# Four attention layers over one adjacency: packing two chunks of signs in one run of TensorE

## What is computed

```python
def _L0_gnn_ref(h, adj, W, a):
    Wh = h @ W
    e = (Wh @ a1)[:, None] + (Wh @ a2)[None, :]
    e = jnp.where(e >= 0, e, ALPHA * e)
    scores = jnp.where(adj > 0, e, NEG_BIG)
    attention = jax.nn.softmax(scores, axis=1)
    return attention @ Wh
...
h = jnp.maximum(_layernorm(x, axis=-1), 0.0)
x = x + _L0_gnn_ref(h, adj, L0_gnn_W, L0_gnn_a)
```

## Time and profile before

| | us |
|---|---|
| median of 3 runs (lowest, highest) | 3853.71 (3852.88, 3855.01) |
| span of the profiled execution | 3851.4 |
| a group of layer 0, pack to pack | 61.05 |
| a group of layer 1, projection to projection | 58.08 |

### The profile page before, as it was taken

One profiled execution on the slowest core, in us unless ns is written; L12 is line 12 of the kernel. 1 busy time (PEld: TensorE's weight loads), 2 busy tenths in 40 slices (PEclk: granted clock), 3 DMA queues, 4 the chain that ended last, 5 costly groups with the idle time before them and its releaser, 6 DMA issues.

```text
span 3851.4 us, 82260 instructions
## 1 busy us (share of the span) xinstructions
PE 3814.9 (99%) x34730; PEld 3789.4 (98%) x34730; DVE 3583.9 (93%) x7818; ACT 1234.0 (32%) x2601; POOL 56.0 (1%) x155
## 2 busy tenths in 40 slices
PE   7999999999999999999999999999999999999999
PEld 7999999999999999999999999999999999999999
DVE  7998999999999999999999999999997999999998
ACT  6777777777631111111133221121123000000000
POOL 4100000000000000000000000000000000000000
PEclk9999999999999999999999999999999999999999
DMA  7988888898300100010002000000000000000000
GB/s 245 303 290 296 295 293 291 289 301 293 127 17 19 18 23 18 18 22 19 15 15 67 18 20 21 18 20 20 18 18 16 15 15 15 15 18 12 15 18 9
DMA packets 223265, 344.00 MB, mean 89 GB/s; under 512 B 72496, under 2 KB 147632, under 8 KB 222896
## 3 DMA queue, kind: packets, MB, share of 16 engines
q1 hardware_dynamic: 221168, 338.48, 28.0%
q10 hardware_dynamic: 1728, 0.27, 0.0%
HBM read 305.70 MB, written 21.20 MB: 85 GB/s over the span
## 4 chain that ended last, share of the span: by engine, by line
PE 96%; DVE 2%; ACT 1%; DMA 1%; issue 1%; DVEq 0%; POOL 0%; ACTq 0%; SPq 0%
PE acc L1360 93%; PE ps_wh L1378 1%; DVE q L855 1%; PE ps_pack L1258 1%; DMA adj_int<-in_adj_dram 0%; ACT adj_pairs L1475 0%; PE ps_pack L1360 0%; DVE mask L799 0%; DMA vals<-in_x_dram 0%; PE acc L1342 0%; PE ps_pack L1244 0%; DVE q L663 0%; PE acc L1288 0%; ACT xnew L1597 0%; PE ps_pack L1265 0%
## 5 line engine op out<-in xcount | busy, mean ns | idle before, releaser
L1360 PE MATMUL acc<-vals,q 128*128 128x129 f32 (+1 forms) x32576 | 3665.7, 275 | 2.4 <-DVE q L855 2.3
L1360 PEld LDWEIGHTS acc<-vals,q 128*128 128x128 f32 x32576 | 3648.5, 192 | 15.3 <-issue 7.5
L855 DVE SCALAR_TENSOR_TENSOR q<-rrow,R,mask 128x512 f32<-128x512 f32 x3968 | 2890.6, 747 | 146.3 <-PE acc L1360 39.5
L1475 ACT ACTIVATE adj_pairs<-adj_int,threshold 128x1024 uint8<-128x1024 int32 x512 | 585.0, 1145 | 214.5 <-PE ps_pack L1258 133.8
L799 DVE TENSOR_SCALAR mask<-bits 128x512 uint16<-128x512 uint16 x2048 | 546.0, 285 | 2.9 <-ACT bits L1485 2.9
L1597 ACT ACTIVATE xnew<-acc,rec 128x128 f32<-128x128 f32 x244 | 69.3, 366 | 862.6 <-DVE rec L893 767.7
L1622 ACT ACTIVATE e<-xnew,nm,rs 128x128 f32<-128x128 f32 x193 | 79.6, 482 | 230.3 <-DVE nm L655 229.5
L1604 ACT ACTIVATE e<-xnew 128x512 f32<-128x512 f32 x47 | 29.6, 631 | 367.7 <-DVE xnew L924 279.7
L1675 ACT ACTIVATE wh<-ps_wh 128x512 f32<-128x512 f32 x48 | 28.7, 598 | 355.0 <-PE ps_wh L1378 354.1
L1617 ACT ACTIVATE sd<-ve 128x4 f32<-128x4 f32 x47 | 9.5, 201 | 353.3 <-DVE ve L635 353.3
L924 DVE SCALAR_TENSOR_TENSOR xnew<-mean,none,xnew 128x128 f32<-128x128 f32 x188 | 64.9, 345 | 47.4 <-ACT xnew L1597 47.4
(11 more groups left out here) (257 smaller groups left out, 829.6 us busy)
## 6 DMA issues: line engine op xcount, KB each, us to landing
adj_int<-in_adj_dram SPq DMA_DIRECT2D x512, 512.0 KB, 4.8
rrow<-rows SPq DMA_DIRECT2D x60, 256.0 KB, 3.3
x_between_layers<-xnew SPq DMA_DIRECT2D x32, 256.0 KB, 2.6
xin<-x_between_layers SPq DMA_DIRECT2D x32, 256.0 KB, 2.8
xin<-in_x_dram SPq DMA_DIRECT2D x16, 256.0 KB, 5.3
wh_of_layer<-wh SPq DMA_DIRECT2D x1, 4096.0 KB, 16.7
x_of_layer<-xnew SPq DMA_DIRECT2D x16, 256.0 KB, 2.3
xin<-x_of_layer SPq DMA_DIRECT2D x16, 256.0 KB, 3.2
```

What stands on the lines that cost most here:

```text
L855: nc.vector.scalar_tensor_tensor(q[:, j % RING, :], row, column(R_, t), mask[:, c % 2, j, :], ALU.max, ALU.mult).then_inc(q_ready, 1)
L1360: last = nc.tensor.matmul(to, q[:, j % RING, b * P:(b + 1) * P], vals[:, t, 0:width(g.layer)], start=first, stop=(t == KT - 1 or g.two and ...
L1475: nc.scalar.activation(adj_bytes[:, n % BIN_RING // 2, :, n % 2], adj_int[:, n % ADJ_RING, :], ACT.Sign, bias=threshold[:, 0:1], accum_out ...
```

## The change

- The ring of signs holds 16 pieces (`BIN_RING`). Odd chunks put theirs into the second half of `mask`, even ones into `adj_pairs` (`pairs_of`). Layer 0's mask has only buffer 0 (`plane_buffer`), so `unpack` also waits until VectorE's own last q is done.
- In groups 1 to 14 of layer 0 TensorE packs two chunks in one run: behind t = 19 chunks 2 and 3 of the group, behind t = 51 chunks 0 and 1 of the next (`RUNS_AT`). Even ones write the bank `ps_pack`, odd ones `ps_bc` (`words_bank`). Group 0 and group 15 pack singly.
- ScalarE copies both chunks' words one behind the other, at i = 0 and i = 16. VectorE turns even chunks at t % 16 == 15, right ahead of their planes, and odd ones at 12 as before.
- In layer 0, but for its last group, `normalised` moves from i = 21 to 23, `copy_hT` from 27 to 28, `copy_wh` from 30 to 31, and TensorE's projection from t = 57 to 50. On SyncE the transposing transfer moves from 25 to 27 and the next rows from 27 to 29.

```diff
-BIN_RING = 8
+BIN_RING = 16
+WORDS_AT = {0: (1, 12, 20, 28), 1: (4, None, None, None), LAST: (None, 12, 20, None)}
+FIRST_SINGLE = GROUPS * CHUNKS - 2
+RUNS_AT = {19: 2, 51: 4}
+RUN_TURN_AT = JC - 1
...
+        def words_bank(C):
+            return ps_bc if C % 2 and FIRST_TURNED <= C < FIRST_SINGLE else ps_pack
...
+        pairs_of = [flat(adj_pairs), flat(mask).bitcast(F16)[:, JC * W // 2:JC * W]]
...
-                    if before and i == 25:
+                    if before and i == 27:
                         turn_halves(before)
-                    if before and i == 27:
+                    if before and i == 29:
                         load_next_rows(before)
...
+                need(dve, q_ready, (g.swept * CHUNKS + c) * JC)
+                planes(bits[:, g.value, c * JC:(c + 1) * JC, :], plane_buffer(g, c)).then_inc(mask_ready, 1)
...
+                        at = RUN_TURN_AT if C % 2 == 0 and C < FIRST_SINGLE else TURN_AT
+                        if FIRST_TURNED <= C < CHUNKS * GROUPS and t % JC == at:
                             turn_words(C)
...
-                need(pe, words_copied, C - FIRST_TURNED)
+                need(pe, words_copied, C - FIRST_TURNED - (C <= FIRST_SINGLE))
...
+                    if g.layer == 0 and 0 < g.value < LAST and t in RUNS_AT:
+                        C = g.value * CHUNKS + RUNS_AT[t]
+                        pack(C // CHUNKS, C % CHUNKS)
+                        pack((C + 1) // CHUNKS, (C + 1) % CHUNKS)
...
-                        if t == (39 if g.two else 57):
+                        if t == (39 if g.two else 50 if g.layer == 0 and not g.last else 57):
                             project(before)
...
+                C = v * CHUNKS + n // QP
+                if n % QP == QP - 2:
+                    need(act, words_turned, C - 1 - FIRST_TURNED)
...
+                    later = g.layer == 0 and not into_last
-                    due.append((2 * QP + 5, lambda: normalised(g)))
-                    due.append((3 * QP + 3, lambda: copy_hT(g)))
-                    due.append((3 * QP + 6, lambda: copy_wh(g)))
+                    due.append((2 * QP + (7 if later else 5), lambda: normalised(g)))
+                    due.append((3 * QP + (4 if later else 3), lambda: copy_hT(g)))
+                    due.append((3 * QP + (7 if later else 6), lambda: copy_wh(g)))
...
+                        if i == 0 and g.value > 1 or i == 2 * QP and 0 < g.value < LAST:
+                            for c in range(2):
+                                words(g.value, i // QP + c)
```

More of the change, by code:

```diff
@@ L804, in planes, with plane_buffer @@
                 return last
+            def plane_buffer(g, c):
+                return 0 if g.layer == 0 else c % 2
             def spread_planes(g, t):
@@ L854, in chunk @@
                     need(dve, q_used, g.swept * KT + t + 1 - RING)
-                    nc.vector.scalar_tensor_tensor(q[:, j % RING, :], row, column(R_, t), mask[:, c % 2, j, :],
+                    nc.vector.scalar_tensor_tensor(q[:, j % RING, :], row, column(R_, t), mask[:, plane_buffer(g, c), j, :],
                                                    ALU.max, ALU.mult).then_inc(q_ready, 1)
@@ L1139, in between @@
                     spread_planes(g, t)
-                    if g.layer == 0 and t % JC == TURN_AT:
+                    if g.layer == 0:
                         C = g.value * CHUNKS + t // JC + 1
-                        if FIRST_TURNED <= C < CHUNKS * GROUPS:
+                        at = RUN_TURN_AT if C % 2 == 0 and C < FIRST_SINGLE else TURN_AT
+                        if FIRST_TURNED <= C < CHUNKS * GROUPS and t % JC == at:
                             turn_words(C)
@@ L1254, in pack @@
                     if C >= FIRST_TURNED:
-                        pairs = adj_pairs[:, i // 2, :].rearrange("p (t b j) -> p b t j", t=PT, b=BLOCKS)
+                        pairs = pairs_of[C % 2][:, i // 2, :].rearrange("p (t b j) -> p b t j", t=PT, b=BLOCKS)
                         half = i // BLOCKS
                         for b in range(BLOCKS):
-                            last = nc.tensor.matmul(ps_pack[b * WORDS:(b + 1) * WORDS, half * 256:(half + 1) * 256],
+                            last = nc.tensor.matmul(words_bank(C)[b * WORDS:(b + 1) * WORDS, half * 256:(half + 1) * 256],
                                                     packer[:, i % BLOCKS // 2, :], pairs[:, b, :, :],
@@ L1364, in chunk @@
                         pack(*FIRST_PACKS[t])
-                    if g.layer == 0 and g.value > 0 and j == JC - 1 and ahead(g.value, c)[0] <= LAST:
+                    if g.layer == 0 and 0 < g.value < LAST and t in RUNS_AT:
+                        C = g.value * CHUNKS + RUNS_AT[t]
+                        pack(C // CHUNKS, C % CHUNKS)
+                        pack((C + 1) // CHUNKS, (C + 1) % CHUNKS)
+                    if g.layer == 0 and g.value == LAST and j == JC - 1 and ahead(g.value, c)[0] <= LAST:
                         pack(*ahead(g.value, c))
@@ L1396, in between @@
                         pe.wait_ge(r_ready, SOON[g.layer + 1].n + 1)
+                        if g.layer == 0:
+                            pe.wait_ge(words_copied, FIRST_SINGLE - FIRST_TURNED)
                         spread(r_early[:, :], ps_bc).then_inc(row_done, 1)
@@ L1481, in words @@
                 act.wait_ge(adj_packed, v * PIECES + (c + 1) * QP)
-                if v * CHUNKS + c >= FIRST_TURNED:
-                    nc.scalar.activation(turned_words, ps_pack[:, :], ACT.Copy, scale=2.0 ** 24).then_inc(words_copied, 1)
+                C = v * CHUNKS + c
+                if C >= FIRST_TURNED:
+                    nc.scalar.activation(turned_words[C % 2], words_bank(C)[:, :], ACT.Copy, scale=2.0 ** 24).then_inc(words_copied, 1)
                     return
@@ L1723, in sweep @@
                             due.pop(0)[1]()
[L1724 to L1727 removed]
+                        at = WORDS_AT.get(g.value, ())
+                        if i in at:
+                            words(*(ahead(g.value, i // QP - 1) if i != at[0] else (g.value, LEAD - 1)))
+                        if i == 0 and g.value > 1 or i == 2 * QP and 0 < g.value < LAST:
+                            for c in range(2):
+                                words(g.value, i // QP + c)
                         v, c = ahead(g.value, i // QP)
```

22 lines of the change are left out of this document (9 added, 13 removed).

## The result

| | before | changed |
|---|---|---|
| median (lowest, highest) | 3853.30 (3852.66, 3855.01), 4 runs | 3889.34 (3886.48, 3892.04), 4 runs |
| span of the profiled execution | 3851.4 | 3889.9 |
| first q matmul of group 0 | 59.81 | 58.81 |
| layer 0, from there to the second full group of layer 1 | 1092.07 | 1132.37 |

The changed kernel is slower by 36.0 us, ratio 1.0093 with a 95% interval of 1.0081 to 1.0105. The forecast was 3863.3 and its range ended at 3875: the sign was right, the size was not, and the time lies outside the range. The profiled execution took 3891.68, 2.3 above the median. In it layer 0 is 40.3 us longer than in before's; the stretches ahead of it and behind it are 1.0 and 0.8 us shorter in these two executions.

A forecast was written before the change was run, and what follows sets the result against it. TensorE, busy for 99% of the span, was taken to bound the kernel. Fewer runs -8.4, waits of before gone -1.6 and the new wait +19.6 sum to +9.6 us: 3863.3 us from 3853.7, range 3843 to 3875.

The forecast's parts named there:

- Part one: TensorE's packs in groups 1 to 14: two double runs replace four single ones, dropping 28 entries, 8.4 us less.
- The entry: TensorE entering and leaving a run of pack matmuls: 0.30 us, paid per run and not per matmul.
- Part two: TensorE's three waits of before, on VectorE's q and the last signs, should all go: 1.6 us less.
- Part three: Second double run, t = 51: TensorE waits 1.4 us for the last piece in 14 groups, 19.6 us more.
- The walk: Timing of one steady group from tile 20: nm at 15.0, last piece wanted at 30.45, TensorE's wait 1.4 us.
- What stays hidden: First double run, t = 19: piece 15 wanted at 18.6, ready at 16.0, 2.6 us early, so no wait.
- Pieces 28 to 31 follow their loads with room: ScalarE's last pieces before the second run's end: their loads land in time, adding no wait.
- The load of piece 27: Issued behind the transposing transfer at 19.14, landing 4.1 us later at 23.25; ScalarE loses 1.0 us.
- Everything behind this wait shifts ...; nothing regained: After TensorE's wait at t = 51 all work moves later by it; other engines regain nothing.
- Loads slower everywhere: Rival: loads behind the transposing transfer take 5.4 us, waits 2.7 a group, 3881 us; chance 0.07.
- No wait at all: Rival: nm 0.5 us sooner and the load landed, TensorE loses nothing at t = 51, 3843.7 us; chance 0.25.
- The entry cost stays: Rival: the 0.30 us comes with each pack, so the 8.4 us saving falls away, 3871.7 us; chance 0.07.

The follow-up runs named there:

- two tiles later: The changed kernel with the second double run behind t = 53 instead of t = 51: 3854.07 us, ratio 1.0002 to before.

## Why the prediction was right and wrong

**Part one, -8.4: right.** The entry was worked out as 0.30 from one interrupted pack and measured as 0.30 between two kernels that differ only in the places of the odd packs. A double pack is busy for 1.05 us (212.20 + 0.61 - 211.76), where 1.06 was forecast. The rule of the Trainium skill ("TensorEngine Tiling (Array Packing)", "Key Properties") that changing the tiling mode drains the engine would give this: the price goes with the run and not with the 16 matmuls. What TensorE does in the 0.30 us no trace here shows.

**Part two, -1.6: right.** The three waits are gone, and VectorE waits for nothing but the ring of q: its only line of more than 0.2 us between 180 and 1000 us is `DVE q L869 <- PE acc L1377`.

**Part three, the wait: the mechanism was right, the size too small.** The walk was made from tile 20, at 468.42 in one group of the profile. `sd` starts at 476.38, that is 7.96 (forecast 7.9), the normalising at 483.42 = 15.0 (15.0), the transposing transfer at 486.28 = 17.86 (17.86). Here are rows of ScalarE's timeline from there on (normalising, pieces 27 and 29), then SyncE's queue and the time to landing of the two loads issued at 487.6 (piece 27's) and 489.7 (piece 29's):

```profile
483.42 1.65 ACT L1647 ACTIVATE e<-xnew,nm,rs 128x128 f32<-128x128 f32 x4 [0.90 <-DVE nm L664]
...
491.85 1.15 ACT L1499 ACTIVATE mask<-adj_int,threshold 128x1024 uint8<-128x1024 int32 x1 [1.06 <-DMA adj_int<-in_adj_dram]
...
496.85 1.15 ACT L1499 ACTIVATE mask<-adj_int,threshold 128x1024 uint8<-128x1024 int32 x1 [0.43 <-DMA adj_int<-in_adj_dram]
```

```profile
486.28 1.23 SPq L481 DMA_TRANSPOSE e<-hT  x1
487.56 1.31 SPq L454 DMA_DIRECT2D adj_int<-in_adj_dram  x2
488.92 0.43 SPq L468 DMA_DIRECT2D xin<-in_x_dram  x1
...
DMA to landing us min/median/max: 4.3/4.3/4.3
...
DMA to landing us min/median/max: 7.1/7.1/7.1
```

In this group piece 27 starts at 23.43 (forecast 23.25) and has lost 1.06 us (1.0). Piece 29's load, issued at 489.7 behind the transfer, two pieces' loads and the next rows, takes 7.1 us to land, and the piece waits 0.43. With that and small gaps TensorE's last four matmuls start at 32.65 (501.07), where 30.45 + 1.4 was forecast.

One group is not the mean, though. `nm` lets ScalarE start at 15.0 in all 13 steady groups, and behind piece 27 the walk is exact in the eight groups where no later load is waited for: 7.27 us to piece 31, as forecast. What differs is loads. Piece 27 waits 0.75 to 2.09 us, 1.28 in the mean, for a forecast of 1.0. The first load behind the transfer landed after 4.0 to 5.2 us, 4.4 in the mean, where 4.1 was taken, and in two groups the transfer held the queue for 2.14 and 2.35 us instead of 1.23. Group 3 shows both (rows of ScalarE and SyncE):

```profile
299.29 1.15 ACT L1499 ACTIVATE mask<-adj_int,threshold 128x1024 uint8<-128x1024 int32 x1 [2.08 <-DMA adj_int<-in_adj_dram]
```

```profile
292.70 2.14 SPq L481 DMA_TRANSPOSE e<-hT  x1
```

The sentence "Pieces 28 to 31 follow their loads with room" failed as well, in four groups of 13, where piece 29, 30 or 31 waits for 0.31 to 1.39 us, 3.0 together. So the step that failed in this part is "The load of piece 27": one landing and one length of the transfer stood for all groups, and that piece's wait was sized at 1.0. The forecast wait was 1.4, the mean is 1.93: 14 x 0.53 = 7.4 us more. Over the 14 groups piece 27's waits are 4.7 us above the forecast and the later pieces' 3.0. The interruptions add 2.7, which I had not priced, although show one: 1007.83 to 1009.49 is 1.66, and less the wait of 0.92 that is 0.74 for a pack that otherwise takes 0.56.

**"What stays hidden": wrong for one group.** The walk of the first run was made for a steady group, with nine pieces left and four lying ready. Group 1 inherits its pieces from group 0, in which nothing lies ready: between 60 and 138 us ScalarE waits 16 times for loads, 17.0 us together. (The share of the DMA engines doesn't tell the two apart: 0.87 to 0.96 in each ten microseconds from 100 to 140, and 0.89 to 0.97 in before.) The kernel before packed C = 7 at 151.03; the changed one wants it at 139. Its last pieces came at 142.7 and 145.2. That is 5.95 us, and 2.6 for the clock.

**"Everything behind this wait shifts ...; nothing regained": incomplete.** The shift itself is right, but a wait of TensorE was priced at its own length. The earlier trace rows showed a granted clock of 1.00, which holds for an engine that never stands still for more than 0.92 us in these groups; it was taken for a constant. The profile of before could have warned. Between two of its layers, where TensorE was busy for 1.9 of the 4 us before 2919.5 (no single wait there over 0.7), the clock falls too, and 32 matmuls take 5.37 us, where 16 of them take 1.95 at 2909.92 (TensorE's timeline, then the window):

```profile
2919.61 5.37 PE L1244 MATMUL ps_pack<-ident 128*128 128x128 f32 x32
...
2920.00:2923.00 3.00, 3.00 (x16) 3.00 (x16) 2.21 (x13) 0.90 (x4) 0.00 (x0) 0.50 0.10 27
```

Here the prediction failed most: the clock was a term put at nothing, and it is 15.5 us, where the result lies 26.0 above the forecast: 7.4 (waits), 2.7 (interruptions), 5.95 (group 1) and 15.5 make 31.6, less 0.9 that the balance has too much, 1.8 outside layer 0, 2.3 from the profiled execution down to the median, and 0.5 by which less time lies around the span than in before. With waits of 1.4 behind the second runs the clock would have cost only group 1's 2.6, since it did not fall behind waits up to 1.78, so the two errors are coupled: half a microsecond more of waiting brought 1.6 more for eight groups of 14.

**The rivals.** "Loads slower everywhere" came nearest in time (3881) and was right in kind, later loads, but piece 27's landed after 5.2 at most, and the waits' mean was 1.93 and not 2.7. "No wait at all" is what two tiles later gives in steady groups. "The entry cost stays" is excluded by the 0.30. The forecast of the wait's name was `ps_pack <- ACT`; it reads `ps_bc <- ACT`, since the second pack of a run writes that bank. The range was too narrow because every bound in it was a bound of the wait alone.

## What to carry to other kernels

A wait that a change adds to the bounding engine can cost more than its own length. Look in the whole profile before for stretches in which that engine worked little, short waits in a row too, and read the granted clock behind them; where a new wait comes near, add the half-clock stretch to the upper bound. Walk a chain with the spread of every landing in it, not with one value. Walk the first groups by themselves whenever work is pulled earlier, since their stores are not yet filled. And where a merge saves tenths but makes the producer late by a microsecond or two, shift its place before judging it: here two tiles were worth 35 us, all but undoing the loss, and with group 1 left alone the merge gained what it promised.

## What the runs showed of the hardware

- After TensorE had stood still for 1.9 to 2.6 us in a stream of fp32 matmuls, the granted clock fell from 1.00 to 0.50 (2.4 to 1.2 GHz) within 1.5 us of its going on, in most cases, and stayed for some 3 us; behind the second runs of the changed kernel that costs 1.5 to 1.6 us and appears as busy time, not as a wait. After up to 1.78 us it did not fall. In group 1, with waits of 3.26 and 2.20, it fell while TensorE stood, and stayed down for some 7 us. In before it fell once between layers without any wait over 0.7 us. Matmuls that nobody reads, put into the wait, kept it up and made the kernel 11.8 us faster. The Trainium skill, page "TensorE: Matmul & The Clock Gate", section "Part 1: The HAM clock gate (the "warmup" mystery)", has these two levels and says that activity releases the lower one; the trace agrees, with 0.50 and 1.00, and the clock is back at 1.00 with TensorE at work (441.00).
- Entering and leaving a run of matmuls on 32 columns within a stream on 128 costs 0.30 us, whether one pack or two stand in the run.
- Of the loads of 512 KB behind a transposing transfer the first landed 4.0 to 5.2 us after issue and the third, with the next rows' load between, 5.5 to 7.4 (14 groups of the changed kernel). A lone load of before took 3.7. The transfer held SyncE's queue for 1.23 us in most groups and for 2.35 at the longest.

Left open: what tells apart the waits between 1.85 and 2.52 us after which the clock fell from those after which it did not; whether the loads are late through the transfer itself or through one another, which no run takes apart; and why layer 0 begins 0.5 to 1.3 us sooner in the changed kernels than in before.
